# Moving a graph convolution's loads and stores in parts of an iteration, and its source rows once

## The reference, cut to what matters

```python
def _L0_gnn_ref(in_feat, src, dst):
    ...
    out_deg = jax.ops.segment_sum(ones, src, num_segments=n)
    in_deg = jax.ops.segment_sum(ones, dst, num_segments=n)
    out_norm = jax.lax.rsqrt(jnp.maximum(out_deg, 1.0))
    in_norm = jax.lax.rsqrt(jnp.maximum(in_deg, 1.0))
    h = in_feat * out_norm[:, None]
    msg = h[src]
    agg = jax.ops.segment_sum(msg, dst, num_segments=n)
    return agg * in_norm[:, None]
...
x = _layernorm(x + _L0_gnn_ref(x, src, dst), axis=-1)
x = _layernorm(x + _L1_gnn_ref(x, edge_index, edge_attr_32, ...), axis=-1)
x = _layernorm(x + _L2_gnn_ref(x, edge_index, ...), axis=-1)
x = _layernorm(x + _L3_gnn_ref(x, src, dst, edge_attr_3, edge_attr_10, edge_weight, ...), axis=-1)
```

## Time and profile before

| | us |
|---|---|
| Median of three runs | 27219.5 (27213.2 to 27268.2) |
| Span of the profiled execution | 31250.7 |
| First and last gather of the convolution's loop, in the profile | 993.2 and 6652.6 |
| Busy in the span: PE, DVE, POOL, ACT | 15884, 15483, 15773, 5202 |

### The profile page before, as it was taken

One profiled execution on the slowest core, in us unless ns is written; L12 is line 12 of the kernel. 1 busy time (PEld: TensorE's weight loads), 2 busy tenths in 40 slices (PEclk: granted clock), 3 DMA queues, 4 the chain that ended last, 5 costly groups with the idle time before them and its releaser, 6 DMA issues. The chain is left out here.

```text
span 31250.7 us, 456719 instructions
## 1 busy us (share of the span) xinstructions
PE 15884.3 (51%) x102440; PEld 9300.4 (30%) x102441; DVE 15483.3 (50%) x31596; ACT 5202.4 (17%) x13760; POOL 15773.3 (50%) x16798
## 2 busy tenths in 40 slices
PE   7344444445555558973000000035777777777776
PEld 5233333333333338861000000022222222222222
DVE  9444444445555554442111115975555555555556
ACT  4111111111111114431000000001222222222222
POOL 0355555556666664442666666722444444444444
PEclk9555555555555555555555555556777777777777
DMA  2444444432222224521223222212444444444443
GB/s 65 100 121 120 120 120 121 119 91 58 58 59 59 58 56 146 154 81 31 82 81 80 80 80 75 72 47 72 92 93 91 92 92 90 93 91 92 92 92 90
DMA packets 2854618, 2738.27 MB, mean 88 GB/s; under 512 B 1309983, under 2 KB 2216029, under 8 KB 2851618
## 3 DMA queue, kind: packets, MB, share of 16 engines
q1 hardware_dynamic: 2287198, 2308.39, 28.2%
q0 software_dynamic: 412544, 241.53, 5.5%
q10 hardware_dynamic: 153668, 172.93, 2.1%
HBM read 2173.27 MB, written 537.90 MB: 87 GB/s over the span
## 5 line engine op out<-in xcount | busy, mean ns | idle before, releaser
L2219 POOL DMA_INDIRECT rows_x<-x_table,index x3125 | 2973.0, 951 | 4269.0 <-DMA index<-in_src 3504.1
L742 POOL DMA_INDIRECT rows<-split_table,index x3125 | 2985.2, 955 | 3665.8 <-DMA index<-in_src 2695.3
L858 POOL DMA_INDIRECT rows<-x_table,index x3125 | 3296.4, 1055 | 1720.6 <-issue 914.5
L1624 POOL DMA_INDIRECT rows_dram<-rows,place_now x3125 | 3025.4, 968 | 2130.5 <-DVE rows L1552 1145.9
L2333 DVE TENSOR_TENSOR second<-banks,h 128x768 f32<-128x768 f32 x2500 | 1949.2, 820 | 1731.5 <-PE banks L2488 1520.0
L1564 PE MATMUL banks<-row_pieces,hot_turned 128*128 x3125 | 390.1, 289 | 4176.5 <-issue 2856.4
L2325 DVE TENSOR_TENSOR first<-banks,h 128x768 f32<-128x768 f32 x2500 | 1969.4, 820 | 1043.5 <-DMA rows_dram<-rows,place_now 399.2
L1552 DVE TENSOR_REDUCE rows<-banks 128x108 f32<-128x324 f32 x1250 | 490.6, 434 | 4022.9 <-issue 2683.7
L550 PE MATMUL banks<-counts,low_turned 128*128 128x98 f32 x6250 | 1810.5, 438 | 427.2 <-ACT counts L538 318.2
L550 PEld LDWEIGHTS banks<-counts,low_turned 128*128 128x128 f32 x6250 | 1614.6, 317 | 556.0 <-issue 525.0
L2463 PE MATMUL banks<-u_turned,w_tensor 32*128 32x384 f32 (+1 forms) x10000 | 1614.3, 545 | 262.5 <-DVE second L2333 206.0
(11 more groups left out here) (479 smaller groups left out, 34278.3 us busy)
## 6 DMA issues: line engine op xcount, KB each, us to landing
key_row<-dst_rows SPq DMA_DIRECT2D x1250, 320.0 KB
h<-hidden_dram SPq DMA_DIRECT2D x1250, 320.0 KB
acc_moved<-dst_rows SPq DMA_DIRECT2D x625, 320.0 KB
src_row<-in_src_rows SPq DMA_DIRECT2D x625, 320.0 KB
hot_turned<-turned_dram SPq DMA_DIRECT2D x1250, 160.0 KB
hot_dram<-onehot SPq DMA_DIRECT2D x625, 160.0 KB
turned_dram<-hot_turned SPq DMA_DIRECT2D x625, 160.0 KB
a_dram<-a ACTq DMA_DIRECT2D x625, 160.0 KB
```

Source lines behind the costliest of these rows:

```text
L742: nc.gpsimd.indirect_dma_start(out=m["rows"][j][:, t * SPLIT:(t + 1) * SPLIT], out_offset=None, in_=m["split_table"], in_offset=bass.Indir ...
L858: nc.gpsimd.indirect_dma_start(out=m["rows"][j][:, t * C2:t * C2 + F], out_offset=None, in_=m["x_table"], in_offset=bass.IndirectOffsetOnA ...
L1624: nc.gpsimd.indirect_dma_start(out=m["rows_dram"], out_offset=bass.IndirectOffsetOnAxis(ap=m["place_now"][j][:, t:t + 1], axis=0), in_=m[" ...
L2219: nc.gpsimd.indirect_dma_start(out=m["rows_x"][j][:, t * F:(t + 1) * F], out_offset=None, in_=m["x_table"], in_offset=bass.IndirectOffsetO ...
```

## The change

An iteration's five groups are divided into two parts (`PARTS`): groups 0 to 2 and groups 3 and 4. `index`, `emb`, `key_row`, `onehot` and `hot_turned` become one tile each, with the groups side by side. Each of the transfers then moves a part at a time: one index load, four embedding loads, one key load and two stores for a part, 16 an iteration. The source rows of an iteration's three groups (two in the next stage) come in one load into one tile.

With it the waits change. SP waits for the gathers of the part's groups of the iteration before, where it waited for `used`, then for the last hidden product of the part, then, ahead of the two stores, for the last `hot_turned` and `onehot` of the part; the key load follows the stores. The source load stands at the end of SP's iteration and waits until all three groups of the iteration before have made `equal`. DVE waits for keys and for finished stores at groups 0 and 3 only, and for the source rows at group 0 only; PE waits for `emb`, and POOL for `index`, at groups 0 and 3 only. POOL still waits for `used` in each group. In the next stage the source load stands after group 2. Sizes and number of the tiles' bytes stay, and so does what is computed.

```diff
@@ -112,6 +112,8 @@
 WIDE = F + 1
 SPLIT = 100
 QUARTERS, QE = 4, T * P // 4
+PARTS = ((0, 3), (3, SLOTS))
+STARTS = [first for first, _ in PARTS]
 
 
 def first_hot(nc, m, g, j):
...
@@ -493,12 +495,13 @@
     def cols(self, i, n):
         return bass.ds((self.first + self.at(i, n)) * T, T)
 
-    def load_sp(self, sp, i, n):
+    def load_sp(self, sp, i):
+
         m, s = self.m, self.s
-        g = self.first + self.at(i, n)
         if not (isinstance(i, int) and i == 0):
-            sp.wait_ge(s["rank_hot"], ONE + self.at(i, n) - self.per + 1)
-        sp.dma_start(m["src_row"][n][:, :], m["src_rows"][bass.ds(g, 1), :].broadcast_to([P, T * P])).then_inc(s["src_row_in"][n], 16)
+            sp.wait_ge(s["rank_hot"], ONE + self.at(i, 0))
+        rows = m["src_rows"][bass.ds(self.first + self.at(i, 0), self.per), :].rearrange("g e -> (g e)").unsqueeze(0)
+        sp.dma_start(m["src_row"][:, :], rows.broadcast_to([P, self.per * T * P])).then_inc(s["src_row_in"], 16)
 
     def hot_dve(self, dve, i, n):
 
...
@@ -507,10 +510,11 @@
         nc.vector.tensor_tensor(cut(m["hot_low"][n][:, :], t=T), rep(m["low"][:, cols], 2, P), rep(self.ramp(P), 1, T), ALU.is_equal)
         nc.vector.tensor_tensor(cut(m["hot_high"][n][:, :], t=T), rep(m["high"][:, cols], 2, NB), rep(self.ramp(NB), 1, T),
                                 ALU.is_equal).then_inc(s["rank_split"], 1)
-        dve.wait_ge(s["src_row_in"][n], 16 * (i + 1))
+        if n == 0:
+            dve.wait_ge(s["src_row_in"], 16 * (i + 1))
         for t in range(T):
             here = slice(t * P, (t + 1) * P)
-            ins = nc.vector.scalar_tensor_tensor(m["equal"][n][:, here], m["src_row"][n][:, here],
+            ins = nc.vector.scalar_tensor_tensor(m["equal"][n][:, here], m["src_row"][:, (n * T + t) * P:(n * T + t + 1) * P],
                                                  m["whole_src"][:, bass.ds((self.first + q) * T + t, 1)], m["before"][:, :],
                                                  ALU.is_equal, ALU.mult)
         ins.then_inc(s["rank_hot"], 1)
...
@@ -583,16 +587,17 @@
     ranks = Ranks(nc, m, s, 0, 5, lambda n: m["ps"][RAMP_BANK][:, 0:n])
 
     def hidden_pe(pe, i, j):
-        pe.wait_ge(s["emb_in"][j], 16 * QUARTERS * (i + 1))
+        if j in STARTS:
+            pe.wait_ge(s["emb_in"][STARTS.index(j)], 16 * QUARTERS * (i + 1))
         pe.wait_ge(s["bent"], ONE + SLOTS * i + j)
         pe.sem_inc(s["going"], 1)
         for q in range(QUARTERS):
             rows = slice(32 * q, 32 * q + EMB)
-            mm = nc.tensor.matmul(m["ps"][0][32 * q:32 * q + 2 * K16, 0:QE], m["w_hidden"][rows, :], m["emb"][j][rows, :], start=True, stop=True)
-        mm.then_inc(s["hidden"][j], 1)
+            mm = nc.tensor.matmul(m["ps"][0][32 * q:32 * q + 2 * K16, 0:QE], m["w_hidden"][rows, :], m["emb"][rows, j * QE:(j + 1) * QE], start=True, stop=True)
+        mm.then_inc(s["hidden"], 1)
 
     def hidden_act(act, i, j):
-        act.wait_ge(s["hidden"][j], ONE + i + 1)
+        act.wait_ge(s["hidden"], ONE + SLOTS * i + j + 1)
         act.wait_ge(s["hidden_out"][j], FULL + 16 * i)
         nc.scalar.activation(m["layer"][j][:, :], m["ps"][0][:, 0:QE], ACT.Relu).then_inc(s["bent"], 1)
         act.wait_ge(s["bent"], ONE + SLOTS * i + j + 1)
...
@@ -626,12 +631,14 @@
             link(nc.vector.tensor_copy(m["ps"][RAMP_BANK][:, 0:P], m["ramp"][:, :]))
 
             def hots(i, j):
-                dve.wait_ge(s["hot_out"][j], FULL + 16 * i)
+                if j in STARTS:
+                    dve.wait_ge(s[f"hot_out{STARTS.index(j)}"], FULL + 16 * i)
                 first_hot(nc, m, SLOTS * i + j, j).then_inc(s["first_hot"], 1)
-                dve.wait_ge(s["key_in"][j], 16 * (i + 1))
-                dve.wait_ge(s["turned_out"][j], FULL + 16 * i)
-                nc.vector.tensor_scalar(m["hot_turned"][j][:, :], m["key_row"][j][:, :], m["part"][:, :], None, ALU.is_equal
-                                        ).then_inc(s["hot_turned"][j], 1)
+                if j in STARTS:
+                    dve.wait_ge(s["key_in"][STARTS.index(j)], 16 * (i + 1))
+                    dve.wait_ge(s[f"turned_out{STARTS.index(j)}"], FULL + 16 * i)
+                nc.vector.tensor_scalar(m["hot_turned"][:, j * T * P:(j + 1) * T * P], m["key_row"][:, j * T * P:(j + 1) * T * P], m["part"][:, :], None,
+                                        ALU.is_equal).then_inc(s["hot_turned"], 1)
 
             def sums(i, j):
                 if 2 <= j < 2 + ranks.per:
...
@@ -694,54 +701,67 @@
             sp.dma_start(m["split_table"].rearrange("(b p) w -> p b w", p=P),
                          m["x_split"][:, :].rearrange("p (b w) -> p b w", w=SPLIT)).then_inc(s["stored"], 16)
 
-            def load(i, j):
-                g = SLOTS * i + j
-                sp.wait_ge(s["used"][j], ONE + i)
-                sp.dma_start(m["index"][j][:, :], m["src"][:, bass.ds(g * T, T)]).then_inc(s["indexed"][j], 16)
-                sp.wait_ge(s["hidden"][j], ONE + i)
+            def load_rows(i, part):
+
+                first, last = PARTS[part]
+                if not (isinstance(i, int) and i == 0):
+                    for j in range(first, last):
+                        sp.wait_ge(s["gathered"][j], 16 * T * i)
+                sp.dma_start(m["index"][:, T * first:T * last], m["src"][:, bass.ds(i * SLOTS * T + T * first, T * (last - first))]
+                             ).then_inc(s["indexed"][part], 16)
+                if not (isinstance(i, int) and i == 0):
+                    sp.wait_ge(s["hidden"], ONE + SLOTS * (i - 1) + last)
+                edges = m["edge_emb"][:, bass.ds((SLOTS * i + first) * T * P, (last - first) * T * P)].rearrange("r (g q e) -> q r g e", q=QUARTERS, e=QE)
                 for q in range(QUARTERS):
-                    sp.dma_start(m["emb"][j][32 * q:32 * q + EMB, :], m["edge_emb"][:, bass.ds(g * T * P + q * QE, QE)]).then_inc(s["emb_in"][j], 16)
-                sp.wait_ge(s["hot_turned"][j], ONE + i)
-                sp.dma_start(m["key_row"][j][:, :], key_row_of(m, g, "dst_rows")).then_inc(s["key_in"][j], 16)
-
-            def store(i, j):
-                g = SLOTS * i + j
-                sp.wait_ge(s["first_hot"], ONE + g + 1)
-                sp.dma_start(m["hot_dram"][bass.ds(g, 1)].rearrange("g p e -> (g p) e"), m["onehot"][j][:, :]).then_inc(s["hot_out"][j], 16)
-                sp.wait_ge(s["hot_turned"][j], ONE + i + 1)
+                    sp.dma_start(cut(m["emb"][32 * q:32 * q + EMB, QE * first:QE * last], t=last - first), edges[q]).then_inc(s["emb_in"][part], 16)
+
+            def load_keys(i, part):
+
+                first, last = PARTS[part]
+                rows = m["dst_rows"][bass.ds((SLOTS * i + first) * T, (last - first) * T), :].rearrange("t e -> (t e)").unsqueeze(0)
+                sp.dma_start(m["key_row"][:, T * P * first:T * P * last], rows.broadcast_to([P, T * P * (last - first)])).then_inc(s["key_in"][part], 16)
+
+            def store(i, part):
+
+                first, last = PARTS[part]
+                here = slice(T * P * first, T * P * last)
+                groups = bass.ds(SLOTS * i + first, last - first)
+                sp.wait_ge(s["hot_turned"], ONE + SLOTS * i + last)
+                sp.wait_ge(s["first_hot"], ONE + SLOTS * i + last)
                 sp.sem_inc(s["going_sp"], 1)
-                sp.dma_start(m["turned_dram"][bass.ds(g, 1)].rearrange("g p e -> (g p) e"), m["hot_turned"][j][:, :]
-                             ).then_inc(s["turned_out"][j], 16)
-            for j in range(SLOTS):
-                load(0, j)
-            for n in range(ranks.per):
-                ranks.load_sp(sp, 0, n)
+                for to, tile, out in ((m["hot_dram"], m["onehots"], "hot_out"), (m["turned_dram"], m["hot_turned"], "turned_out")):
+                    sp.dma_start(to[groups].rearrange("g p e -> p g e"), cut(tile[:, here], t=last - first)).then_inc(s[f"{out}{part}"], 16)
+            for part in range(len(PARTS)):
+                load_rows(0, part)
+                load_keys(0, part)
+            ranks.load_sp(sp, 0)
             with sp.Fori(1, ITERS) as i:
-                for j in range(SLOTS):
-                    load(i, j)
-                    store(i - 1, j)
-                    if j < ranks.per:
-                        ranks.load_sp(sp, i, j)
-            for j in range(SLOTS):
-                store(ITERS - 1, j)
+                for part in range(len(PARTS)):
+                    load_rows(i, part)
+                    store(i - 1, part)
+                    load_keys(i, part)
+                ranks.load_sp(sp, i)
+            for part in range(len(PARTS)):
+                store(ITERS - 1, part)
             halves_sp(sp, m, s, W)
             sp.wait_ge(s["stored"], 16)
-            for j in range(SLOTS):
-                sp.wait_ge(s["hot_out"][j], FULL + 16 * ITERS)
-                sp.wait_ge(s["turned_out"][j], FULL + 16 * ITERS)
+            for part in range(len(PARTS)):
```

(14 more changed lines are left out.)

## The result

The changed kernel takes 27288.7 us in the median of 11 runs (27248.9 to 27419.0); the kernel before takes 27200.2 beside it. The ratio is 1.0036, with a 95% interval of 1.0024 to 1.0047: slower by 88 us (65 to 128), where 220 us were forecast.

The account below looks back on a forecast made before the run. POOL's floor, 31.2 us an iteration, was taken to bound the convolution; a 3.4 us source-row stall lifts the 29.6 us loop to 33.0. 1.8 us x 124 = 223 us on 27219.5 gives 27440 us, range 26950 to 27800.

Parts of the forecast that it names:

- What bounds the stage: Convolution: slow stretches read as a recording cost; outside them POOL's floor of 31.2 us an iteration bounds it.
- The walk of the loop of DVE and PE: Convolution: one round of the DVE and PE loop summed to 29.6 us, 1.6 us under POOL's floor.
- Fewer issues: SP in the convolution: 17 issues an iteration instead of 43, saving 11 us of SP's time, covered by its idle time.
- The source rows: Convolution: one late load makes DVE wait 2.9 to 3.8 us an iteration, 3.4 taken; loop grows to 33.0 us.
- 2240 KB take 12.0 to 12.8 us: SP's queue in the convolution: time for stores, keys and source rows, at 213 to 243 KB a us plus a fixed part.
- A margin of 1.6 us: Convolution: POOL's floor of 31.2 us ahead of the 29.6 us loop; a stall must pass it to show.
- POOL's floor covers it: Rival, convolution: the stall stays hidden, no change, 27220 us; chance 0.31 together with the change doing nothing.
- The rival of the index wait: Convolution: POOL's index wait, 13.6 us an iteration, is partly on the path; faster, 26820 us; chance 0.20.
- the change does not do what it says: Rival: merged transfers keep their row length and land as late, 27220 us; chance 0.31 together with the covered case.
- The next stage: Stage after the convolution, two groups' source rows in one load: 0, bounded by 80 us either way.

Follow-up runs that it names:

- before_4g: The kernel before with four gathers a group instead of five in the convolution: 26979.4 us, convolution 29.47 us an iteration.
- after_4g: The changed kernel with four gathers a group instead of five in the convolution: 27236.1 us, convolution 30.83 us an iteration.
- first_only: The kernel before with only the next stage's two source rows loaded together after group 2: 27153.1 us, ratio 0.9998.
- after_nop6: The changed kernel with six one-element memsets on DVE ahead of the next stage's loop: 27231.3 us, ratio 1.0005 to the kernel before.
- before_nop122: The kernel before with 122 one-element memsets on DVE ahead of the next stage's loop: 27341.8 us, ratio 1.0056.
- after_both: The changed kernel with the next stage's ramp, and the second operand of equal in both stages, in PSUM: 26895.7 us, ratio 0.9888 to the kernel before.
- conv_only: The kernel before with the change in the convolution alone, the next stage's source rows loaded as before: 27363.4 us, ratio 1.0074.
- before_nop10: The kernel before with ten one-element memsets on DVE ahead of the next stage's loop: 27281.9 us, ratio 1.0016.

## Why the prediction was wrong, point by point

**What bounds the stage: right.** The stretches of the earlier trace rows were no part of the kernel, as read there, though that recording caused them is not shown; without them the convolution runs at POOL's pace, 31.6 us an iteration where 31.2 was worked out from the earlier trace rows. The walk of the loop of DVE and PE gave 29.6, and before_4g measured 29.47.

**Fewer issues: right.** SP issues 17 an iteration, and merged ones take little longer than the others: the key load most, 0.50 us in the median instead of 0.36. The second part's share of one iteration of the changed kernel on SP, then the hidden product that it waits for and the `equal` that waits for it:

```profile
3016.15 0.37 SPq L710 DMA_DIRECT2D index<-in_src  x1
3019.67 1.74 SPq L716 DMA_DIRECT2D emb<-in_edge_emb  x4
3021.69 0.42 SPq L733 DMA_DIRECT2D hot_dram<-onehots  x1
3022.21 0.42 SPq L733 DMA_DIRECT2D turned_dram<-hot_turned  x1
3022.72 0.46 SPq L722 DMA_DIRECT2D acc_moved<-dst_rows  x1
3023.45 0.42 SPq L504 DMA_DIRECT2D src_row<-in_src_rows  x1
```

```profile
3018.70 0.75 PE L596 MATMUL banks<-emb,w_hidden 10*32 10x160 f32 x8
...
3029.59 0.66 DVE L511 TENSOR_TENSOR hot_high<-high,banks 128x490 bf16<-128x490 f32 x1
3032.14 1.40 DVE L517 SCALAR_TENSOR_TENSOR equal<-src_row,acc,before 128x128 bf16<-128x128 int32 x5 [1.89 <-DMA src_row<-in_src_rows]
```

**The source rows: the mechanism right, the size wrong, and this is the first step that failed.** The chain is the one described. Its cover, from the hidden product to the end of `hot_high`, was forecast at 10.8 us; here `hot_high` ends at 3030.25 and the hidden product at 3019.45, 0.22 ahead of the first embedding load: 10.8. But the term "2240 KB take 12.0 to 12.8 us" was too large: from the first store, 3021.69, to `equal` at 3032.14 it is 10.45. (Over 119 iterations of this trace the median is 10.6, from 9.9 to 11.4.) The rate of 213 to 243 KB a us came from one pair of transfers of another stage. With 10.45 in its place, the stall is 1.4 us instead of 3.4 (1.89 in these rows: the embedding loads hold the first store back by 2.02 us, not 1.74), the loop 31.0 instead of 33.0 (30.83 in after_4g), and the sum itself says "covered". The estimate from the Trainium skill, DMA: Bandwidth & Descriptors, "Anatomy of one DMA", 7.3 us for the same bytes, is 3.2 us too short, further off than the 1.6 to 2.4 of the term. A margin of 1.6 us was set against a difference of two numbers over 10 us that was not known to within 2.

**So the first rival, POOL's floor covers it, is what happened in the convolution:** 8 us in the traces where 223 were forecast. The rival of the index wait fell: in the kernel before, recorded again, POOL's wait for the index in the stage is 18.9 us in 62 waits, not 13.6 us an iteration. That the change does not do what it says fell as well: by the pages the busiest DMA queue moves the same 2308 MB in 2098186 packets instead of 2287198, and one load serves the source rows of an iteration, with one wait.

**The next stage: the second step that failed.** "0, bounded by 80 us either way" was argued from its source load, and as far as that goes it was right (first_only, 0.9998). The 126 us came from something that the prediction did not look at: that stage's gathers were at POOL's pace already, two of them an iteration were already held by DVE's second SBUF operand, and the convolution's shorter list of DVE instructions moved the loop to a place where one is held longer. The held gathers were to be seen in the first recording, too; the reading stopped at the stage that the change was about.

So the sign came out as forecast by luck, through another mechanism in another stage. Of the two parts, this study shows each apart: the convolution's stall is covered, and after_nop6 and before_nop122 move the loss off the change and onto the kernel before.

## What to carry to other kernels

When POOL's gathers set the pace, look at the length of each beside what DVE does at that moment: here one operand moved from SBUF to PSUM took 1.0 to 1.1% off the time of the kernel before, whichever of the two kernels it was moved in. A stall matters only by what it exceeds of the pace that bounds the loop, so price it from two sides and compare with that margin; if the margin lies inside the uncertainty, the honest forecast is "covered or not". And when a change shifts the instructions of a loop that it does not touch, a difference of some tenths of a per cent may be that loop's new place: add a few idle instructions and measure again before the change is blamed or praised.

## What the runs showed of the hardware

- A gather that overlaps `hot_low` with two SBUF operands takes 1.7 to 3.6 us in nearly every iteration, instead of 0.944. With one operand of these DVE instructions in PSUM the longest is 957 ns (after_both).
- How long the second of an iteration is held depends on where the DVE instructions stand in DVE's list: it ends 2.2 us after the first one's start at the places 742, 752 and 800, and 3.2 at 736, 738 and 864.
- One recorded execution was 4031 us longer than the median and hid which engine bounds a stage: 45.3 us an iteration in one recording of a kernel, 31.60 in the next.
- Left open: the executions of conv_only but for the profiled one lie 66 to 89 us above that one (27288.4), and most of before_nop10 50 us above its own; their traces do not show where.
